# Quartered second block, earlier stores, and one diagonal block moved behind a turn, in a four-layer graph kernel

## The reference

```python
# layer 1: users (rows 0..2047) and items (the rest) have their own diag, par and W
e = par[0] * par[1] * (diag[:, None] * x @ W) + x
h = adj @ (adj.T @ e)
layer1 = layernorm(h) * gamma + beta + x
# layer 2
layer2 = 1.0 - 0.1 * x - 0.01 * sum(x * (adj @ x), axis=1, keepdims=True)
# layer 3
deg = clip(sum(adj, axis=1) + 1, 1)
z = relu(concat([x, (adj @ x + x) / deg]) @ W2 + b2)
layer3 = z / max(norm(z), 1e-12)
# layer 4: Chebyshev, K = 4
T0 = x; T1 = adj @ T0; T2 = 2 * adj @ T1 - T0; T3 = 2 * adj @ T2 - T1
layer4 = T0 @ w[0] + T1 @ w[1] + T2 @ w[2] + T3 @ w[3] + bias
```

## Time and profile before

| | us |
|---|---|
| median of 3 runs | 1519.48 |
| lowest, highest | 1519.17, 1523.22 |
| the profiled execution | 1519.97 |
| its span, first to last instruction | 1518.1 |
| PE busy | 1494.2 |
| DVE, ACT, POOL busy | 611.6, 251.7, 61.3 |
| mean granted TensorE clock | 0.994 |

### The profile page before, as it was taken

The page is one execution under the profiler, slowest core; times in us unless marked ns, Lnnn a source line. Parts: engine busy times, 40 slices in busy tenths (PEclk is TensorE's granted clock), DMA queues, the critical chain, the costliest instruction groups (busy, mean ns, idle before and its releaser), DMA issues.

```text
span 1518.1 us, 17598 instructions
## 1 busy us (share of the span) xinstructions
PE 1494.2 (98%) x6638; PEld 695.4 (46%) x6638; DVE 611.6 (40%) x1335; ACT 251.7 (17%) x492; POOL 61.3 (4%) x66
## 2 busy tenths in 40 slices
PE   8999999999999999999999999999999999999998
PEld 5555555555555533334444344443444444444332
DVE  4755565655555567433332544233111021110432
ACT  3333334333333410000100001000000000000000
POOL 0000000000000012100000110010000000000010
PEclk9999999999999999999999999999999999999999
DMA  9899999999999999999888488886488868988996
GB/s 302 322 392 409 412 409 413 410 409 413 411 408 412 358 364 384 421 422 397 302 307 300 176 333 302 297 291 241 145 330 312 305 227 343 336 321 297 371 413 260
DMA packets 122483, 519.11 MB, mean 342 GB/s; under 512 B 21116, under 2 KB 21156, under 8 KB 72356
## 3 DMA queue, kind: packets, MB, share of 16 engines
q1 hardware_dynamic: 105312, 412.64, 72.5%
q10 hardware_dynamic: 17092, 105.38, 16.6%
HBM read 411.82 MB, written 106.17 MB: 341 GB/s over the span
## 4 chain that ended last, share of the span: by engine, by line
issue 99%; POOLq 0%; POOL 0%; DVE 0%
POOL power_out L433 0%; POOLq L431 0%; POOLq L433 0%; DVE rows L922 0%; POOL ident L426 0%; POOLq L428 0%; POOL ident L428 0%; POOLq L1165 0%
## 5 line engine op out<-in xcount | busy, mean ns | idle before, releaser
L748 PE MATMUL ps_u<-blk,vectors 128*128 128x512 f32 (+1 forms) x1984 | 720.5, 596 | 1.1 <-DMA blk<-a_transposed 1.1
L748 PEld LDWEIGHTS ps_u<-blk,vectors 128*128 128x128 f32 (+1 forms) x1984 | 287.8, 172 | 386.2 <-issue 381.2
L485 ACT ACTIVATE blk<-ps_turn 128x512 f32<-128x512 f32 x400 | 206.3, 605 | 330.6 <-PE ps_turn L566 326.4
L607 PE MATMUL ps_h<-blk,u_rows 128*64 128x512 f32 x720 | 164.4, 598 | 0.0
L1087 DVE TENSOR_TENSOR part<-part,ps_u 64x512 f32<-64x512 f32 (+1 forms) x45 | 30.9, 686 | 317.1 <-PE ps_u L748 316.2
L838 DVE TENSOR_REDUCE row_part<-blk 128x4 f32<-128x2048 f32 x68 | 152.4, 2279 | 0.1
L822 DVE TENSOR_TENSOR part<-part,ps_h 128x512 f32<-128x512 f32 x80 | 55.0, 688 | 186.3 <-PE ps_h L607 186.3
L566 PE MATMUL ps_turn<-ident,blk 128*128 128x128 f32 x1072 | 126.7, 277 | 3.4 <-DMA blk<-in_adj 3.4
L566 PEld LDWEIGHTS ps_turn<-ident,blk 128*128 128x128 f32 x1072 | 118.2, 142 | 23.7 <-issue 19.5
L590 PE MATMUL ps_u<-blk,e 128*64 128x512 f32 x544 | 124.3, 596 | 0.0
L433 POOL TENSOR_TENSOR power_out<-power_in,minus_half 128x4 f32<-128x4 f32 x60 | 60.6, 1010 | 1453.2 <-DVEq L885 1453.2
(11 more groups left out here) (118 smaller groups left out, 577.0 us busy)
## 6 DMA issues: line engine op xcount, KB each, us to landing
blk<-a_transposed SPq DMA_DIRECT2D x287, 1024.0 KB, 6.4
a_transposed<-blk ACTq DMA_DIRECT2D x100, 1024.0 KB, 10.0
blk<-in_adj SPq DMA_DIRECT2D x67, 1024.0 KB, 22.5
nat_far<-in_adj SPq DMA_DIRECT2D x32, 1024.0 KB, 22.1
early_blk<-a_transposed SPq DMA_DIRECT2D x4, 1024.0 KB, 16.2
rows<-in_x SPq DMA_DIRECT2D x10, 128.0 KB, 9.3
out<-rows SPq DMA_DIRECT2D x10, 128.0 KB, 3.6
blk<-in_adj SPq DMA_DIRECT2D x4, 256.0 KB, 3.7
```

What stands on the lines that cost most here:

```text
L485: nc.scalar.activation(blk[:, n % RING, t, :], ps_t[t][:, :], ACT.Copy)\
L607: mm = pe.matmul(ps_h[n % 2][half(t), :], u_rows[:, t, :], blk[:, n % RING, t, :], start=t < 2, stop=t >= TB - 2)
L748: mm = pe.matmul(acc, left, tiles[:, t, :], start=first, stop=last)
```

## The change

There are three edits.

1. `IN_QUARTERS = 2`: block 1 too is loaded in four quarters, and PE turns it by `turn_quarters`, which is `turn_first` with the block's number: for each quarter four transposes, one into each bank, with a wait on `at_evacuated` ahead of the first transpose into each bank. DVE waits for the quarters of block 1 ahead of its work on it.
2. `LATE = 6`: the first two stores come at n = 7, two more at n = 9, and the lag has gone at n = 60.
3. The block (1,8,8) is moved behind (1,9,9), and `turn(2,0)` is now done in its middle. So `add_own(1,8)` becomes the `meanwhile` of `end_l2` of row (2,0), `add_y(2,1)` becomes its `at_last`, and `add_y(2,2)` comes behind it. The counts that were worked out from (s, r) now come from the order of the list (`n_own`, `n_own_added`).

```diff
-    LATE = 8
+    LATE = 6
+    IN_QUARTERS = 2
...
-                    diagonal([r - 1])
+                    if s + 1 != LATE_HEAD:
+                        diagonal([r - 1])
...
             then("turn", s + 1, 0, mid)
+            if s + 1 == LATE_HEAD:
+                diagonal([NB - 2])
...
+        own_order = [(s, r) for b in sorted(after) for what, s, r in after[b] if what == "keep"]
+        def n_own(s, r):
+            return own_order.index((s, r)) + 1
+        def n_own_added(s, r):
+            return sum(k in in_both for k in own_order[:n_own(s, r)])
...
-                if n == 0:
+                if n < IN_QUARTERS:
                     for c in range(TB - 1):
-                        sp.dma_start(nat(0)[:, c, :], a_blocks[:, c, 0:BLK]).then_inc(quarter_loaded[c], 16)
-                    sp.dma_start(nat(0)[:, TB - 1, :], a_blocks[:, TB - 1, 0:BLK]).then_inc(nat_loaded[0], 16)
+                        sp.dma_start(nat(n)[:, c, :], a_blocks[:, n * TB + c, 0:BLK]).then_inc(quarter_loaded[n][c], 16)
+                    sp.dma_start(nat(n)[:, TB - 1, :], a_blocks[:, n * TB + TB - 1, 0:BLK]).then_inc(nat_loaded[n], 16)
...
-            def turn_first():
+            def turn_quarters(n):
                 for c in range(TB):
                     if c < TB - 1:
-                        pe.wait_ge(quarter_loaded[c], 16)
+                        pe.wait_ge(quarter_loaded[n][c], 16)
                     else:
-                        pe.wait_ge(nat_loaded[0], 16)
+                        pe.wait_ge(nat_loaded[n], 16)
                     for t in range(TB):
-                        mm = pe.transpose(ps_t[t][:, c * P:(c + 1) * P], nat(0)[:, c, t * P:(t + 1) * P], ident[:, :])
+                        if c == 0 and n > 0:
+                            pe.wait_ge(at_evacuated, TB * (n - 1) + t + 1)
+                        mm = pe.transpose(ps_t[t][:, c * P:(c + 1) * P], nat(n)[:, c, t * P:(t + 1) * P], ident[:, :])
...
-                    if what == "keep" and (s, r) in in_both:
+                    if what == "keep" and (s, r) in in_both and (s, r) != (LATE_HEAD - 1, NB - 2):
                         add_own(s, r)
...
-                            ENDS[s](i, n, lambda: add_y(LATE_HEAD, 1), at_last=lambda: add_y(LATE_HEAD, 2))
+                            ENDS[s](i, n, lambda: add_own(LATE_HEAD - 1, NB - 2), at_last=lambda: add_y(LATE_HEAD, 1))
+                            add_y(LATE_HEAD, 2)
```

More of the change, by code:

```diff
@@ L164, in build @@
         nat_loaded = [sem(f"nat_loaded{k}") for k in range(NAT)]
-        quarter_loaded = [sem(f"quarter_loaded{c}") for c in range(TB - 1)]
+        quarter_loaded = [[sem(f"quarter_loaded{n}_{c}") for c in range(TB - 1)] for n in range(IN_QUARTERS)]
         nat_summed = sem("nat_summed")
@@ L612, in _ @@
                 pe.transpose(ps_h[1][:, k % TB * P:(k % TB + 1) * P], ident[:, :], ident[:, :])
-            turn_first()
+            turn_quarters(0)
             turn_x_in(0)
@@ L617, in _ @@
             for n in range(NB):
-                turn_block(n + 1)
+                if n + 1 < IN_QUARTERS:
+                    turn_quarters(n + 1)
+                else:
+                    turn_block(n + 1)
                 if n + 1 < NB:
@@ L856, in _ @@
             make_e(0)
-            for c in range(TB - 1):
-                dve.wait_ge(quarter_loaded[c], 16)
             for n in range(NB):
+                for c in range(TB - 1) if n < IN_QUARTERS else ():
+                    dve.wait_ge(quarter_loaded[n][c], 16)
                 if n + 1 < NB:
```

20 lines of the change are left out of this document (10 added, 10 removed).

## The result

| | before | after |
|---|---|---|
| median of the runs, us | 1519.46 (13 runs) | 1516.15 (13 runs) |
| lowest, highest | 1515.00, 1524.75 | 1513.83, 1519.17 |
| profiled execution, us | 1519.97 | 1516.15 |
| its span, us | 1518.1 | 1514.4 |

The ratio is 0.9975, with a 95% interval of 0.9963 to 0.9987: 3.8 us faster (2.0 to 5.6). The forecast was 1514.8 us, in a range of 1511.9 to 1518.6.

A forecast was written before the change was run, and what follows sets the result against it. PE was taken as the bound, busy 1494.2 of the 1518.1 us span. Terms of -3.5 (start), +0.8 (earlier stores) and -2.0 us (diagonal block) took 1519.5 to 1514.8 us; range for 8 in 10 runs 1511.9 to 1518.6.

The forecast's parts named there:

- A: Whole kernel: the sum of the three edits' terms as it stands, 1514.8 us; chance 0.42.
- B: Start: the clock falls all the same, so the start gives 2.2 us and the kernel takes 1516.1 us; chance 0.20.
- Edit 1, predicted -3.5 or -2.2: Start: block 2 is turned 3.5 us earlier by quarters, or 2.2 us if the clock falls.
- the last quarter lands with the last byte of the block, near 13.0: Start, block 1: the last quarter still lands near 13.0 us, leaving four transposes, 0.5 us at full clock.
- block 2 lands at 16.5: Start: block 2's load lands at 16.5 us, so its turning starts then instead of at 20.19.
- the small allowance: Start, SP: three more issues ahead of block 2 delay it only a little, so 3.5 us is taken instead of 3.7.
- 12 of the 16 transposes are done at full clock while the last quarter is under way: Start, block 1: 12 transposes, 1.5 us, fill PE's gap in 8 to 12 us, to about 2.9 of 4 us busy.
- Edit 2, predicted +0.8, bounds -1.9 to +3.4: First part: earlier stores bring a 2.7 us wait at block 25 and remove 1.9 us at block 35, net +0.8 us.
- rival E: First part: loads starve behind stores, 8.6 us wait at block 25 and a clock fall, +2.9 us, 1522.4 us; chance 0.10.
- I count the lead in full: First part: loads and stores move with PE, so the 3.5 us won at the start all survives.
- D: First part: full DMA engines eat the start's lead, leaving only the diagonal block's gain, 1517.5 us; chance 0.17.
- Edit 3, predicted -2.0: Diagonal block: waits of 1.3 and 0.85 us replace 2.60 us, no half clock, block (2,1,1) starts 2.0 us earlier.

The follow-up runs named there:

- held lag: The changed kernel with the stores' lag kept at six blocks until block 38, then falling by one each nine blocks: 1510.95 us, ratio 0.9946.
- The 16 at the start: The changed kernel with 16 unused transposes of the identity added right before PE turns block 1: 1517.19 us in one run.
- held lag with filling: The held lag on the changed kernel, plus unused identity transposes at the start, 6 before the first piece of x, 16 before block 1: 1512.95 us, ratio 0.9952.

## Why the prediction was right, and where its sum was off

**Which case.** The time of A (1514.8) is 1.35 us from the median, that of B (1516.1) 0.05 us. That B is so near is chance: its price for the start, -2.2 us, is not what the trace shows (-3.17). The trace has B's mark in weak form: the clock fell, but for half the time. Against the profiled execution the sum was -4.7 us and -3.8 was measured (1519.97 to 1516.15). The three terms came out at -3.17, +2.4 and -1.81, which is -2.6 in all, so each won less or cost more than predicted. What brought the result back near the forecast is about 1.1 us of small gains that the sum did not have. The places were foreseen; that the time fits so well is luck in part.

**Edit 1, predicted -3.5 or -2.2.** -3.17 in the trace. Alone it is -3.3 us in the ratio. That it comes out between the two is luck in part: the start differs from run to run. With one transfer block 2 was turned at 20.19, 16.40, 17.42 and 20.86 us in four traces; with quarters and no filling at 17.02, 15.93, 15.37, 19.71, 15.34, 15.65, 16.07 and 15.53 in eight. The means are 18.7 and 16.3, 2.4 us apart. The step "the last quarter lands with the last byte of the block, near 13.0" held (13.1), and "block 2 lands at 16.5" too (16.56). Block 2 was issued 2.5 us later than before (7.0 us, not 4.5), but took 9.5 us instead of 12.0, so the small allowance for this was right. The step that failed is that 12 of the 16 transposes are done at full clock while the last quarter is under way: the first quarter came only at 11.1 us, since with other transfers in flight the quarters took 8 us each, not the 3 that the first block's took the earlier trace rows. The 16 transposes took 3.27 us, most of them at half clock (until 13.9). Of the 1.5 us of transposes that were to come into 8 to 12 us little did: PE was busy for 1.99 us there (1.44 before, 2.9 predicted). In the other traces with quarters and no filling the first quarter landed earlier and the clock stayed up, but for that of the held lag, where a piece of x came late.

The Trainium skill says in "TensorE: Matmul & The Clock Gate", section "Part 4: PE-mode transpose", that a transpose does not count as PE being busy in the way a multiply does. One run speaks against it for these f32 transposes: 28 of the identity in the wait at block 25, and the clock stayed at 1.00 where it fell without them. The 16 at the start decide nothing, since it stayed up in most runs without them. And the earlier trace rows show the rise only by the durations (421 ns, then 273): the granted clock that the profile gives is 1.00 in all of 0 to 8 us, also where the transposes take 421 ns. The prediction left this out.

**Edit 2, predicted +0.8, bounds -1.9 to +3.4.** The mechanism was right: a wait of 2.60 us at block 25 (predicted 2.7), none at block 35, the gap at 40 to 60 us filled. Missing in the sum is the clock behind the wait: 3.4 us at half rate, 1.7 us. Only rival E had it. I had the row that asked for it, 0.57 behind the 2.60 us wait, and priced a wait of the same length without it. So what stands at these two blocks is 2.60 + 1.7 - 1.9 = +2.4, which by chance is also what edit 2 costs alone (2.4, from 0.8 to 4.3). But it is not shown to be all edit 2's: without it the traces with quarters wait at block 25 too (4.15 and 1.96 us), and by the ratios edit 2 takes 1.4 us on top of the other two, with intervals that overlap.

**"I count the lead in full."** This is the step that failed most. The prediction argued that loads and stores move with PE. They were issued earlier, but the load of block 25 landed at 135.6 in the changed kernel and at 135.9 before, since it took 29.6 us instead of 26.8. Edits 1 and 3 without the early stores also wait there, for 1.96 us with the half clock behind. So the wait is no matter of edit 2 alone, and D was partly right: of the lead of 3.17 us, 1.0 was left at the last turn, where the prediction asked for 2.7. But its reason, that the engines are full, was not: with the lag held they are as full (1.03), and nothing is lost.

**Edit 3, predicted -2.0.** -1.81, from 1.66 at `times_x` to 3.47 at (2,1,1). The waits were 1.60 and 1.02 us, predicted 1.3 and 0.85; no half clock, as predicted. But that hangs by little: in two other traces with the same wait (held lag, and held lag with filling) the clock fell, and the edit gave 1.2 us, near the prediction's bound of 1.3; in the trace of edit 3 alone it was 0.85. The row end took 7.5 us (856.66 to 864.2), not 7.4. The wait ahead of turn(2,1) is 0.3 us longer than predicted because `add_y(2,1)` is over and the turn begins 7.23 us behind the start of the row's end (I had 7.05), and PE is through its blocks 5.63 us behind it (I had 5.75).

**Small terms.** About 0.3 us in the first part, 0.6 us at the loads of the second part, where two waits of 1.1 us in all are now one of 0.5, and 0.2 us behind (2,1,1) were not in the sum.

**The three edits together.** By the ratios the three alone give -3.3, +2.4 and -3.2, in all -4.1; the three together give -3.8. Within these intervals they add up.

## What to carry to other kernels

Where DMA engines are full, their busy share says little: it was 1.03 with the wait and without it. Look at what stands ahead of the one load that comes next, spread stores evenly, and let no step of a lag put three of them in one place. Price a wait of about 2 us on TensorE with the half clock behind it (1.7 us here) before calling the sum done. A start that wins time makes the next tight load the bound, so look for that load before counting a lead in full.

## What the runs showed of the hardware

- Holding the stores' lag on top of the change gives 1510.95 us, 8.2 us (0.54%) below the kernel before and below the changed kernel's 1516.15: the best version of this study.
- The wait ahead of turn(2,1) was 1.59 to 1.61 us in eight traces. The clock fell behind it in two of them (held lag, and held lag with filling) and stayed up in six. Behind 1.9 us at block 35 it stayed up, behind 1.96 us at block 25 it fell. The fall makes the 24 entries 1.7 us longer; 0.6 us is left of it at (2,1,1), since the wait of 1.02 us there goes. This is a part of why runs of one kernel differ by several us.
- 28 transposes of the identity in a wait at block 25 kept the clock at 1.00 (one trace); seven waits of 1.96 us or more at that place brought it down.
- Of two loads issued at 104.3 us, one landed after 28.9 us and the other after 22.7, at the same DMA share. In the first part of edit 1 alone and that of edits 1 and 3, which are the same, the load of block 25 took 31.1 and 28.9 us, and PE waited 4.15 and 1.96. Why it moves so much between runs of one schedule was not settled; with the held lag it took 21.8 to 23.2 us in four traces, with the falling one 26.5 to 31.5 in ten.
- Block 1 had landed whole between 11.5 and 13.9 us in the traces, and a piece of x landed 3 us late once. Why was not tried.
